# Constant products added to TensorE's order, while the last groups of a six-stage decoder run

## The reference

```python
x = _layernorm(x + _L0_attn_ref(x, ...))            # windowed attention, 16 heads, window 7
x = _layernorm(x + _L0_xattn_ref(x, ctx, ctx, ...)) # cross attention on a context
x = _layernorm(x + _L0_ffn_ref(x, ...))             # 8 experts, each picks 16 of 128 tokens
x = _layernorm(x + _L1_attn_ref(x, ...))            # attention with a decay mask
x = _layernorm(x + _L1_xattn_ref(x, ctx, ...))      # choose one context row per token, attend over them
x = _layernorm(x + _L1_ffn_ref(x, ...))             # w1, depthwise convolution over time, silu, w2
```

## Time and profile before

| | |
|---|---|
| median of 3 runs | 1041.53 us |
| profiled execution | 1041.03 us |
| its span, first to last instruction | 1039.2 us |
| mean granted TensorE clock | 0.963 |
| TensorE busy | 923.8 us, 89% of the span |
| VectorE busy | 863.0 us, 83% |
| ScalarE busy | 745.8 us, 72% |
| GpSimd busy | 208.7 us, 20% |
| products on TensorE | 7382 |

### The profile page before, as it was taken

The page is one execution under the profiler, slowest core; times in us unless marked ns, Lnnn a source line. Parts: engine busy times, 40 slices in busy tenths (PEclk is TensorE's granted clock), DMA queues, the critical chain, the costliest instruction groups (busy, mean ns, idle before and its releaser), DMA issues.

```text
span 1039.2 us, 20265 instructions
## 1 busy us (share of the span) xinstructions
PE 923.8 (89%) x7382; PEld 673.1 (65%) x7382; DVE 863.0 (83%) x2215; ACT 745.8 (72%) x1857; POOL 208.7 (20%) x469
## 2 busy tenths in 40 slices
PE   6788999999999999999999999999999988887552
PEld 4566666767676776767776767677676756565331
DVE  5897668698989989898999899999989885868755
ACT  2385666787877777787877777777878787767643
POOL 2011211214131212213131312122131312111010
PEclk9989999999999999999999999999999999999765
DMA  8922220200203030202103030303011000000000
GB/s 271 376 70 79 71 74 18 77 16 27 85 4 109 1 112 1 87 26 68 45 21 92 8 104 2 112 1 96 17 51 51 21 1 21 1 22 1 11 10 11
DMA packets 36628, 59.06 MB, mean 57 GB/s; under 512 B 6656, under 2 KB 15872, under 8 KB 36016
## 3 DMA queue, kind: packets, MB, share of 16 engines
q1 hardware_dynamic: 36528, 57.76, 17.7%
HBM read 28.77 MB, written 4.19 MB: 32 GB/s over the span
## 4 chain that ended last, share of the span: by engine, by line
PE 57%; ACT 19%; DVE 14%; issue 4%; POOL 3%; SPq 1%; DMA 1%; ACTq 0%; POOLq 0%; DVEq 0%
PE bank_c L463 17%; PE bank_a L463 8%; PE banks_e L463 8%; PE bank_x L463 6%; PE bank_f L463 3%; DVE neg_top L1251 3%; ACT squares_out L1385 3%; PE bank_x L672 3%; ACT area_e L1600 3%; PE banks_e L841 2%; DVE x L927 2%; DVE area_f L1311 2%; ACT area_bx L1373 2%; ACT area_f L1634 2%; PE bank_a L569 2%
## 5 line engine op out<-in xcount | busy, mean ns | idle before, releaser
L1311 DVE SCALAR_TENSOR_TENSOR area_f<-area_f,w_convw 128x254 f32<-128x254 f32 x256 | 111.9, 479 | 12.2 <-ACT area_f L1634 10.5
L1251 DVE TENSOR_REDUCE neg_top<-banks_e 128x8 f32<-128x1024 f32 x64 | 76.6, 1222 | 13.7 <-PE banks_e L463 13.4
L1373 ACT ACTIVATE area_bx<-bank_x 128x512 f32<-128x512 f32 (+1 forms) x144 | 70.1, 498 | 24.3 <-PE bank_x L463 9.6
L1634 ACT ACTIVATE area_f<-area_f,w_convb,w_convw 128x256 f32<-128x256 f32 x128 | 69.7, 594 | 15.6 <-DVE area_f L1302 15.4
L1104 DVE TENSOR_TENSOR area_a<-area_a 128x512 f32<-128x512 f32 x112 | 74.6, 685 | 1.3 <-DMA area_a<-area_a 0.2
L1049 DVE TENSOR_TENSOR area_a<-area_a 128x512 f32<-128x512 f32 x112 | 73.0, 687 | 2.0 <-PE bank_a L569 1.5
L1600 ACT ACTIVATE area_e<-banks_e 128x512 f32<-128x512 f32 x128 | 68.5, 599 | 5.6 <-PE banks_e L841 5.2
L1108 DVE TENSOR_TENSOR area_a<-area_a 128x512 f32<-128x512 f32 x96 | 65.8, 686 | 0.3
L1373 ACT ACTIVATE area_a<-bank_a 128x512 f32<-128x512 f32 (+1 forms) x80 | 44.2, 553 | 22.9 <-PE bank_a L463 18.0
L1373 ACT ACTIVATE area_bx<-bank_c 128x512 f32<-128x512 f32 x64 | 34.5, 539 | 30.3 <-PE bank_c L463 24.2
L463 PE MATMUL bank_x<-area_bx 128*128 128x128 f32 (+1 forms) x256 | 52.3, 337 | 4.4 <-ACT area_bx L1373 2.7
(11 more groups left out here) (318 smaller groups left out, 2587.2 us busy)
## 6 DMA issues: line engine op xcount, KB each, us to landing
area_a<-area_a SPq DMA_DIRECT2D x96, 224.0 KB
area_a<-in_xT SPq DMA_DIRECT2D x16, 256.0 KB, 3.0
area_bx<-in_ctxT SPq DMA_DIRECT2D x16, 256.0 KB, 2.8
x<-in_x SPq DMA_DIRECT2D x16, 256.0 KB, 3.7
area_d<-in_ctxT SPq DMA_DIRECT2D x16, 256.0 KB, 2.7
y<-x SPq DMA_DIRECT2D x16, 256.0 KB, 2.2
w_wqkv_e<-in_wqkv_e SPq DMA_DIRECT2D x1, 3072.0 KB, 10.4
area_f<-in_raw SPq DMA_DIRECT2D x2, 1024.0 KB, 12.1
```

The costliest lines, as they stand in the source:

```text
L1251: dve.tensor_reduce(top[:, b, r:r + 2, :, 0].rearrange("p r (par c) -> p r c par", c=DC), banks_e[:, r:r + 2, :].rearrange("p r (c par k) ...
L1311: last = dve.scalar_tensor_tensor(c4[:, i, :, dst], h4[:, i, :, src], cwt3[:, 2 * jj + i, k:k + 1], c4[:, i, :, dst], ALU.mult, ALU.add)
L1373: return act.activation(dst, src, ACT.Copy)
L1634: last = act.activation(c4[:, i], h4[:, i], ACT.Identity, bias=w["convb"][:, j:j + 1], scale=cwt3[:, j, 1:2])
```

## The change

A new station W (warm) of 186 steps is added on TensorE. Its first step waits until the last group's X station has been added to x (n_x.added); each step then makes one product of ones_bf with the first tile of bias_parts, read twice over, which is 128x512 in bf16, into bank_x. Nobody reads it. The numbers of the stations start at one occurrence for W, as for S.

The strings of DVE, ACT, POOL and SP are the same. TensorE's string is the same once the letters W are taken out. The W stand as follows. Nine come before the projection of D of the last group (950.28 us in the trace of before), four before the transposition that begins at 955.84 us. Of groups 15 and 16 of E and F, the numbers before a step, by its start in the trace of before, are:

| start, us | step | W before it |
|---|---|---|
| 965.51 | scores, second half | 7 |
| 966.88 | row scales | 4 |
| 968.04 | transposition of quantized input | 5 |
| 970.35 | transposition of maxima | 3 |
| 971.82 | logits | 3 |
| 974.18 | w1, second | 4 |
| 976.39 | values | 5 |
| 978.26 | w1, third | 1 |
| 979.09 | transposition back | 2 |
| 980.99 | logits | 5 |
| 982.25 | w1, fourth | 6 |
| 987.14 | values | 13 |
| 989.79 | transposition back | 5 |
| 991.58 | transposition of maxima | 6 |
| 992.12 | transposition | 2 |
| 993.16 | row scales | 1 |
| 993.92 | output projection | 2 |
| 997.23 | w2 | 1 |
| 1003.55 | last group: row scales | 12 |
| 1004.83 | transposition | 5 |
| 1006.63 | w1, first | 3 |
| 1008.45 | w1, second | 12 |
| 1012.00 | w1, third | 12 |
| 1015.56 | w1, fourth | 17 |
| 1025.38 | transposition of maxima | 27 |
| 1026.96 | row scales | 4 |
| 1028.52 | w2, first piece | 5 |
| 1028.9 and later | w2, second piece | 1 |

```diff
--- before.py
+++ after.py
@@ -36,6 +36,7 @@
 W2 = DC * T
 HID = 1024
 HJ = HID // P
+WARM = 186
 NJ = HJ // 2
 
 SLIDE = 24
@@ -75,8 +76,9 @@
         "BXEFBEACXEAXCQCXEXCEFXQCXECEXEDFAXEDFDXDADDFEFBFEFXBXBQBFXBAEXEBFACEXCXAECECXQXCFECEXDXFQDEXDXEDAXFDADQE"
         "FBXFEFBFBXBEXFAEXFAEBABEQCXCXQCECXFXEXECXCEXDXFAEDADXDFDQDAEXFBFEFBXFEBXBFEBXBAFEACXEXQCECXCXEXCEXCEXDXF"
         "EFDQXDAFDADDFQEXFBEFBXFBABFEXEBXFBAEAXCCXECECFXXDXCFECEXBEXEDXFDXDAFADFDFXEXBEBXFBXEBFBFECXEXCXECEXCFXEC"
-        "EFXCXEDXEFDXDDFFDDFXEFCXCECFCXFXCECEDXEXEXEXDFXFXEDEXEDEDFDECCFEFCFCEFECCFEFDEDEDEDFEEFDEDFEEFFEFEFEFEEF"
-        "EEFEFEFFFFFFFFFFFFF"
+        "EFXCXEDXEFDXDDFFDDFXEFCXCECFCXFXCECEDXEXEXEXDFXFXEDEXEDEDFDECCFEFCFCEFECCFEFDEDEWWWWWWWWWDEDFEWWWWEFDEDF"
+        "EWWWWWWWEWWWWFWWWWWFWWWEFWWWEWWWWFWWWWWEWFWWEWWWWWEWWWWWWFWWWWWWWWWWWWWEWWWWWEWWWWWWFWWEWFWWEWFWWWWWWWWW"
+        "WWWFWWWWWFWWWFWWWWWWWWWWWWFWWWWWWWWWWWWFWWWWWWWWWWWWWWWWWFWWWWWWWWWWWWWWWWWWWWWWWWWWWFWWWWFWWWWWFWFFF"
     ),
     "DVE": (
         "SQQQSSSQSASSSASASSSSSSSSSSSSAASAAAAAAAAAASSAAAASSSSSAAAAQSQQQSSSSSSSSSASASASSSSSASSSSSSSBBAASSSSSAAABAAA"
@@ -151,7 +153,7 @@
 def walk(order, stations):
 
     done, live = object(), {}
-    left = {name: iter(range(1 if name == "S" else NG)) for name in stations}
+    left = {name: iter(range(1 if name in "SW" else NG)) for name in stations}
     for name in order:
         if name not in live or next(live[name], done) is done:
             live[name] = stations[name](next(left[name]))
@@ -914,7 +916,13 @@
                 last.then_inc(f_out, 1)
                 yield
 
-            walk(ORDER["PE"], {"S": setup, "Q": queries, "A": windowed, "B": cross, "X": experts, "C": decayed, "D": choose, "E": memory, "F": feed_forward})
+            def warm(_):
+                pe.wait_ge(n_x.added, NG)
+                for i in range(WARM):
+                    pe.matmul(bank_x[:, :], ones_bf[:, :], bc(bias_parts[0][:, :], 1, GB), start=True, stop=True)
+                    yield
+
+            walk(ORDER["PE"], {"W": warm, "S": setup, "Q": queries, "A": windowed, "B": cross, "X": experts, "C": decayed, "D": choose, "E": memory, "F": feed_forward})
```

## The result

Five runs of the changed kernel have a median of 1035.57 us (1035.03 to 1037.93), five of the kernel before beside them 1042.04 us. The ratio is 0.9938, with a 95% interval of 0.9923 to 0.9953. The profiled execution took 1035.57 us with a span of 1033.8. The part ahead of the change took 0.55 us longer in it than in the profiled execution of before (0.42 of that in the first 24 us), so I compare from one step that both have and that the change does not move: the value product near 941 us. From its start to the first addition of the last group to x are 1032.13 - 941.15 = 90.98 us before and 1026.67 - 941.70 = 84.97 us after. That is 6.01 us less, and the sum in the prediction was 6.0.

A forecast was written before the change was run, and what follows sets the result against it. The tail was taken as bound by a hand-over between TensorE, VectorE and ScalarE, with TensorE steps at half clock. Savings of 6.0 us gave 1035.5 against the median 1041.53; one fall added 1.6, forecast 1037.0, range 1034.6 to 1040.0.

The forecast's parts named there:

- the sum in the prediction: From 948 us to the end: 3.26 + 0.95 + 0.6 + 1.3 - 0.1 = 6.0 us saved.
- 3.26 + 0.95: Groups 15 and 16 bring w2 3.26 us earlier; two steps before the last group's first evacuation save 0.95.
- The cover of the late w1 products: Last group: late w1 products still reach VectorE 0.6, 1.1 and 0.6 us in time; without that, 1.2 us each at most.
- the gap arithmetic: Start-to-start time of real steps, less the first's streaming at full clock, against added products of 0.216 us each.
- the case with one fall: Clock falls at one of two remaining gaps: 1035.5 + 1.6 = 1037.1, rounded 1037.0 us; chance 0.40.
- the two gaps: Idle times left before the last group's row scales (2.0 us) and transposition of maxima (1.9 us), where the clock may fall.
- the rival without a fall: Clock falls at neither remaining gap in the last group: 1035.5 us; chance 0.25.
- The price of a fall: Added products and real steps run slow: 1.5 us at the row scales, 1.7 us at the transposition of maxima.
- constants do not hold the clock: After 966 us, products of constants fail to hold the clock as real ones do; slower, about 1080 us; chance 0.07.
- the other engines absorb the gain: Clock holds, but VectorE and ScalarE orders absorb the TensorE gain from 966 to 997 us: 1037 to 1040; chance 0.13.
- The slower mechanism: After 966 us added products at 0.43 us make TensorE the bound: about 39 us later, 1080; half of chance 0.07.
- The page's rule: Skill page lets bursts stand further apart before the clock is lost; neither last-group gap would cost anything: 1035.5 us.

The follow-up runs named there:

- products up to group 15: Changed kernel with added products only through the w2 step of group 15 (88 of 186), none in the last group: 1040.65 us, ratio 0.9969.
- the last group alone: Changed kernel with added products only from the last group's row scales on (98 of 186): 1040.89 us, ratio 0.9972.
- the fall at 942: Changed kernel with eight more products before the value product near 941 us and eight instead of nine before the projection after it: 1036.41 us, ratio 0.9929.
- the zeros: Changed kernel with both operands of the added products taken from a tile of zeros: 1036.78 us, ratio 0.9943.
- the wider gaps: Changed kernel with six instead of twelve products before the last group's row scales, eighteen instead of twenty-seven before its transposition of maxima: 1039.62 us, ratio 0.9961.
- half width: Changed kernel with every added product 256 columns wide instead of 512, same 186 places: 1039.06 us, ratio 0.996.
- doubled products: Changed kernel with twice the added products in the last group (196 instead of 98): 1053.42 us, ratio 1.0102.
- the gaps filled: Changed kernel with the remaining idle times before five TensorE steps filled, 211 added products in all: 1036.35 us, ratio 0.9939.

## Why the prediction was right, and where it was not

*The sum.* By the points at which the prediction stopped, each as the distance from the value product, before and after:

- second logits (980.99 and 979.85): 1.69 us earlier, 1.6 predicted;
- copy of the second value product (989.14 and 987.26): 2.43, 2.1 predicted. ScalarE took it right behind its tanh, as the prediction had;
- w2 product of group 15 (997.23 and 994.40): 3.38, 3.26 predicted;
- first evacuation of the last group (1007.71 and 1004.01): 4.25, against 3.26 + 0.95 = 4.2;
- first quantization (1027.69 and 1023.49): 4.75, against 4.8;
- first addition (1032.13 and 1026.67): 6.01, against 6.0.

Inside these the nine products before the projection cost 0.25 instead of 0.13, in part since they began 0.1 us after the logits had streamed and the projection was ready before they were through. The two experiments that split the change measured its two parts at 3.3 and 2.6 us in their traces, so that they add up is shown there and not only argued. The timed runs are coarser: 3.2 (2.0 to 4.4) and 2.9 (1.5 to 4.4), with the bare medians 2.5 and 2.2.

*A reading of the earlier trace rows was wrong.* The prediction takes the evacuation at 1011.26 as one beside a busy TensorE. In the trace of before TensorE was idle then too, from 1009.49 to 1012.00. So nothing there showed that a busy TensorE leaves VectorE's reads of PSUM alone. The changed kernel does: the evacuation at 1007.57 lies beside twelve added products, which begin at 1006.84, and takes 0.68 us.

*The cover of the late w1 products.* Predicted 0.6, 1.1 and 0.6 us in time; they end at 1007.00, 1010.03 and 1014.14, and VectorE takes them at 1007.57, 1011.12 and 1014.67: 0.6, 1.1, 0.5. Doubling the products took this cover away and cost what the gap arithmetic said.

*The forecast itself, 1037.0, was the case with one fall, and this was wrong; that the time lies in the range does not make it right.* The step that failed is "Both lie at the length after which the clock fell (1.93) and above the one after which it did not (1.65)". In the four profiled executions that have them (the changed kernel, the last group alone, the fall at 942, the zeros) the idle times of 1.82 to 1.83 and 1.72 to 1.75 us left the clock up all eight times; at those of 3.11 and 3.67 us it fell. Filling the two gaps gained nothing. So the rival without a fall (1035.5) was the right case, and its number was the measured median. What I took as evidence, one fall after 1.93 us, was a weak reason. In the traces of before, of the changed kernel and of the products up to group 15 the clock fell at once behind that value product; in those of the last group alone, the wider gaps and the zeros it fell 5 to 6 us after the value product's start, behind further short pauses; in those of half width and of doubled products it did not fall at all. The idle time ahead of it was 1.92 to 1.94 us each time. The length of one gap does not decide it. The trace of before had shown this already, at a place that the prediction does not look at:

```profile
848.03 1.06 PE L463 MATMUL banks_e<-area_e,chosen_v 128*32 128x512 f32 x8 [1.13 <-ACT area_e L1600]
849.81 0.91 PE L463 MATMUL bank_x<-area_bx 128*128 128x128 f32 x4 [0.71 <-ACT area_bx L1373]
850.78 3.37 PE L463 MATMUL bank_c<-area_c,w_qk 128*128 128x256 f32 x8
```

The clock was down from 850.1 to 853.6 us, and no pause just ahead of it is longer than 1.13 us. The same fall is in the traces of the changed kernel, of the products up to group 15 and of the gaps filled, and in none of the other six. What else decides the runs don't settle. In the last group the work around the gap is without a pause, and near 941 and 850 us it is not (a further wait follows), but that this is the reason is only argued.

*The price of a fall* was right in kind: 1.5 and 1.7 us were predicted, 1.47 and 2.26 measured in the kernel with wider gaps. The mis-sized term is the second. The first w2 product started 4.72 us after the transposition (1028.81 - 1024.09) instead of 2.67, so 2.05 of the 2.26 us are in the nine products and the two real steps ahead of it. All of them ran slow, because this fall lasted longer: in the first the clock was down from 1002.2 to 1005.7 us, in the second from 1022.7, still in the pause, to 1029.6. Nine products at 0.43 instead of 0.216 are 1.9 us more. In the run with half the width the fall at this place lasted as long (1022.4 to 1029.3).

*The rivals.* That constants do not hold the clock is refuted, for zeros too. That the other engines absorb the gain is refuted by the run with products up to group 15. The slower mechanism, TensorE becoming the bound, was made real by doubling and has its price: of 21.2 us added in the last group 4.6 found room, and past the room in front of a step every added product costs its 0.216 us.

*The page's rule.* The prediction named the Trainium skill, "TensorE: Matmul & The Clock Gate", section "Why this matters for your kernels", as speaking for the case without a fall. For the two gaps of the last group the trace agrees with it. For the pause of 2.21 us in the run with half the width, and that of 1.93 in the kernel before, it does not: the clock fell behind both, and at 850 us with no pause over 1.13.

## What to carry to other kernels

Where a kernel ends in a hand-over between engines, look at the granted clock of its last slices: TensorE steps that take twice their usual length on that path are a gain that products of constants can bring back, here 6 us of 1042, if a PSUM bank is free. Put in as many as fit between the starts of two real steps at the full clock, less the first one's streaming time, and let a real step be late only where its reader is later still. The pauses of 1.7 to 1.8 us left in the last group did no harm in four executions, and filling them gained nothing, so the last of the room need not be filled; that such a pause is harmless elsewhere is not shown. Too few products bring the fall back, and with full-width ones the last group then took longer than with none (36.00 us against 34.95); too many cost their whole length.

## What the runs showed of the hardware that I had not expected

- Products of zeros by zeros hold TensorE's clock as well as others: 75.60 us against 75.59 for the same stretch.
- The same pause at the same step gave different falls in different executions. The changed kernel and the runs "up to group 15", "wider gaps" and "twice the products" have the same order on TensorE up to 995 us and the same 1.93 us pause ahead of the value product; the clock fell at 942.8 and 943.2, at 947.6, and not at all. A fall at 947 instead of 943 made the projection come 1.08 us later. Where the rest of the spread between runs of one kernel comes from is not shown, but much of it can lie ahead of the tail: in the eight executions with nothing added before it, the value product started between 941.04 and 943.31 us.
- Near 950 us added products did not make a fall dearer. From the value product near 941 us to the next one are 10.79 us without a fall (twice the products in the last group), 12.28 with a fall at 947 and the nine products in it (953.83 - 941.55), and 12.98 with a fall at 949 and no products (956.29 - 943.31, the last group alone). In that last one TensorE paused 1.62 us in the middle of the fall and the clock was down from 949.1 to 956.1 us, where with the products it was back at 951.1. So what a fall costs depends on the place: products in front of real steps delay them, and where they fill a pause the clock seems to come back sooner. That is one or two executions of each, and no more than a hint.
